# Router logits of two expert stages computed inside the preceding attention; flag rows written from two queues

## The reference, cut to what matters

```python
x = x + L0_xattn(layernorm(x), ctx, ctx)          # stage l0a: 16 heads of 16
x = x + L0_ffn(layernorm(x))                      # stage l0f: 8 experts, best one
x = x + L1_xattn(ctx, layernorm(x))               # alignment by dynamic programming
x = x + L1_ffn(layernorm(x))                      # stage l1f
x = x + L2_xattn(layernorm(x), ctx)               # stage l2a: rotary, 16 heads
x = x + L2_ffn(layernorm(x))                      # stage l2f: 8 experts, best two
x = x + L3_xattn(layernorm(x), ctx, ctx, topk=32) # stage l3a
x = x + L3_ffn(layernorm(x))                      # stage l3f: attention over flagged tokens

def expert_ffn(x, Wr, br, W1, b1, W2, b2):        # x: 2048 tokens, already normalised
    logits = x @ Wr + br                          # 2048 x 8: the router
    gates, idx = ...                              # softmax at the best one (l0f) or over the best two (l2f)
    for e in range(8):
        y_e = gelu(x @ W1[e] + b1[e]) @ W2[e] + b2[e]
    return sum of gate * y_e over the chosen experts
```

## Time and profile before

| what | value |
|---|---|
| time, median of 3 runs | 2520.89 us (2513.68 to 2522.03) |
| the profiled execution's own time | 2515.29 us |
| its span | 2513.5 us |
| mean granted TensorE clock | 0.819 of full |
| PE busy | 2020.0 us (80%) |
| PEld busy | 1639.0 us (65%) |
| DVE busy | 1603.9 us (64%) |
| ACT busy | 1173.2 us (47%) |
| POOL busy | 948.7 us (38%) |

### The profile page before, as it was taken

One profiled execution on the slowest core, in us unless ns is written; L12 is line 12 of the kernel. 1 busy time (PEld: TensorE's weight loads), 2 busy tenths in 40 slices (PEclk: granted clock), 3 DMA queues, 4 the chain that ended last, 5 costly groups with the idle time before them and its releaser, 6 DMA issues. The chain is left out here.

```text
span 2513.5 us, 40472 instructions
## 1 busy us (share of the span) xinstructions
PE 2020.0 (80%) x13332; PEld 1639.0 (65%) x13332; DVE 1603.9 (64%) x5245; ACT 1173.2 (47%) x3284; POOL 948.7 (38%) x906
## 2 busy tenths in 40 slices
PE   8995899599948967776999946777777877774887
PEld 5664798599837855555999935566666666662564
DVE  6765111588974246753111169999999999992784
ACT  3552232455321114432333326677787777771443
POOL 3310454300006023302555435666666666651110
PEclk9996899755879988987999966676777777777899
DMA  3111575520305012323454330010010000002342
GB/s 94 64 56 59 205 246 178 150 33 1 134 17 176 0 63 75 102 70 126 149 197 162 103 120 24 1 38 9 30 38 10 30 30 1 30 30 105 127 152 68
DMA packets 104533, 207.81 MB, mean 83 GB/s; under 512 B 20334, under 2 KB 72455, under 8 KB 96391
## 3 DMA queue, kind: packets, MB, share of 16 engines
q1 hardware_dynamic: 80520, 119.75, 14.5%
q0 software_dynamic: 23808, 85.50, 9.9%
HBM read 217.99 MB, written 56.92 MB: 109 GB/s over the span
## 5 line engine op out<-in xcount | busy, mean ns | idle before, releaser
L802 DVE MATCH_REPLACE8 l3a_left<-l3a_top,l3a_left 128x256 f32<-128x256 f32 x768 | 312.4, 420 | 0.0
L795 DVE MAX8 l3a_top<-l3a_left 128x8 f32<-128x256 f32 x768 | 289.5, 424 | 0.0
L507 POOL TENSOR_TENSOR l3a_prob<-l3a_expd,l3a_rest 128x512 f32<-128x512 f32 x128 | 162.5, 1270 | 208.3 <-ACT l3a_rest L589 207.4
L362 PEld LDWEIGHTS l3a_psO<-l3a_probT,l3a_vp 128*128 128x128 f32 x1024 | 177.6, 258 | 71.0 <-ACT l3a_probT L605 41.4
L362 PE MATMUL l3a_psO<-l3a_probT,l3a_vp 128*128 128x128 f32 x1024 | 201.3, 358 | 27.0 <-ACT l3a_probT L605 27.0
L344 PE MATMUL l3a_psT<-all_ident,l3a_prob 128*128 128x128 f32 x512 | 110.0, 354 | 109.6 <-POOL l3a_prob L507 109.0
L494 POOL TENSOR_TENSOR l3a_kept<-l3a_raw_sc,l3a_mone 128x512 f32<-128x512 f32 x128 | 163.2, 1275 | 70.6 <-ACT l3a_raw_sc L573 63.6
L1821 ACT ACTIVATE l2f_hT<-l2f_psH,l2f_wt 128x128 f32<-128x128 f32 x312 | 89.2, 368 | 213.3 <-PE l2f_psH L1752 213.3
L500 POOL TENSOR_TENSOR l3a_sc_sb<-l3a_kept,l3a_mlow 128x512 f32<-128x512 f32 x128 | 164.6, 1286 | 10.0
L2183 PE MATMUL dtw_psS<-dtw_r,all_shift 128*128 128x1 f32 x596 | 152.9, 357 | 10.1 <-DVE dtw_r L2363 9.7
L344 PEld LDWEIGHTS l3a_psT<-all_ident,l3a_prob 128*128 128x128 f32 x512 | 78.3, 182 | 126.5 <-POOL l3a_prob L507 126.3
(11 more groups left out here) (545 smaller groups left out, 4815.6 us busy)
## 6 DMA issues: line engine op xcount, KB each, us to landing
key_at<-l3a_a_k SPq DMA_DIRECT2D x8, 768.0 KB, 3.3
o_at<-l0a_oraw SPq DMA_DIRECT2D x16, 256.0 KB, 2.0
l0a_osum<-o_at SPq DMA_DIRECT2D x32, 128.0 KB
kv_at<-dtw_vd SPq DMA_DIRECT2D x8, 512.0 KB, 2.8
k_at<-dtw_kx SPq DMA_DIRECT2D x8, 512.0 KB, 4.0
l1f_kx<-k_at SPq DMA_DIRECT2D x8, 512.0 KB, 4.6
kv_at<-l1f_k SPq DMA_DIRECT2D x8, 512.0 KB, 3.2
l2a_k<-kv_at SPq DMA_DIRECT2D x8, 512.0 KB, 5.8
```

The lines of the kernel that those rows point to most:

```text
L362: mm = nc.tensor.matmul(psO[y % 2][:, c, 0:P], vp[:, p, kc, c, g * P:g * P + P], probT[:, u % 2, kc, e, :], start=(j == 0 and e == 0 and k ...
L507: nc.gpsimd.tensor_tensor(prob[:, u % 4, :, :], expd[:, u % 2, :, :], rest[:, u % 2, :, :], ALU.subtract).then_inc(picked, 1)
L795: ins = nc.vector.max(top[:, e, eight], rows[:, e, :] if r else scores[:, e, :])
L802: ins = nc.vector.match_replace(out=rows[:, e, :], in_to_replace=top[:, e, eight], in_values=rows[:, e, :] if r else scores[:, e, :], imm_ ...
```

## The change

Both `paired_attention` calls in front of an expert stage get `route`: shared tiles for mean and variance (`mv`) and raw logits (`lg_raw`), and the router's weights. Right behind `add_out` of batch g (slot 4g + 14) DVE makes the statistics of its two tiles and subtracts the mean (`row_moments`); in slot 4g + 15 PE turns the rows (`rows_turned`) and ACT copies them (`read_rows`); in slot 4g + 17 PE multiplies by the router's weights (`routed`) and DVE copies the 16 columns (`read_routes`). The loop becomes three slots longer, and the ring of banks gets the uses "fx" and "fl". The expert stage takes the root and reciprocal of all deviations at once, multiplies the raw logits by it and adds the bias; ACT makes the normalised rows from `x`, `rstd` and an offset; the gates are formed later. In l3f, `n_w` no longer counts the four small constants: they are issued ahead of batch 1's loads and waited for as `m_in`; `w_in` (with `wo`) is waited for by PE only in slot 14. In l3a the 16 flag DMAs are split between SP and ACT.

```diff
@@ picked_attention, sync / scalar
+        def flag_rows(queue, what, first, done):
+            parts = ahead[what].rearrange("b p (e c n) -> b p e c n", c=DC, n=S)
+            for f in range(2):
+                row = ahead["flags"][first + f:first + f + 1, :]....to_broadcast([B, P // 32, S])
+                for e in range(2):
+                    for c in range(DC):
+                        queue.dma_start(parts[:, DK * (1 - e) + 1 + f:P:32, e, c, :], row).then_inc(done, 16)
...
-            for what, f in (("q", 0), ("q", 1), ("k", 2), ("k", 3)):
-                for e in range(2):
...
-            sp.wait_ge(flagged, 16 * 17)
+            flag_rows(sp, "q", 0, q_flagged)
+            sp.wait_ge(q_flagged, 16 * 8)
...
+            act.wait_ge(flagged, 16)
+            act.wait_ge(a_out[(B - 1) % 2], 48 * (B // 2))
+            act.wait_ge(a_out[B % 2], 48 * (B // 2))
+            flag_rows(act, "k", 2, k_flagged)
+            act.wait_ge(k_flagged, 16 * 8)
@@ paired_attention
-    LAST = NQ + 11
+    LAST = NQ + (11 if route is None else 14)
...
-        n_w = 1 + len(Br) + (4 if groups is not None else 0)
+        n_w = 1 + len(Br)
...
+            if route is not None:
+                turns += [[], [("fl", (n - 17) // 4)], [], [("fx", (n - 15) // 4)]][t]
...
                 sp.dma_start(mk[:], groups[2:4, :]).then_inc(m_in, 16)
+                for n, t in (("sel", rg_sel), ("own", rg_own), ("fold", rg_fold), ("one", rg_one)):
+                    sp.dma_start(t[:], w[n]).then_inc(m_in, 16)
...
+            def rows_turned(g):
+                out = take("fx", g)
+                pe.wait_ge(xc_set, g + 1)
+                for c in range(DC):
+                    for t in range(QT):
+                        mm = nc.tensor.transpose(out[:, c, t * P:t * P + P], xc[:, t, c * P:c * P + P], ident[:])
+                mm.then_inc(fx_ps, 1)
+
+            def routed(g):
+                out = take("fl", g)
+                pe.wait_ge(fx_ev, g + 1)
+                if g == 0:
+                    pe.wait_ge(r_in, 16)
+                for t in range(QT):
+                    mm = product(out[:, 0, t * E:t * E + E], [xcT[:, c, t * P:t * P + P] for c in range(DC)], [wr_sb[:, c, :] for c in range(DC)])
+                mm.then_inc(fl_ps, 1)
...
-            pe.wait_ge(w_in, 16 * n_w)
-            if groups is not None:
-                pe.wait_ge(m_in, 16)
+            if groups is None:
+                pe.wait_ge(w_in, 16 * n_w)
             for n in range(LAST):
                 b, t = divmod(n, 4)
+                if groups is not None and n == 1:
+                    pe.wait_ge(m_in, 16 * 5)
+                if groups is not None and n == 14:
+                    pe.wait_ge(w_in, 16 * n_w)
...
+                if route is not None and t == 3 and 0 <= (n - 15) // 4 < B:
+                    rows_turned((n - 15) // 4)
+                if route is not None and t == 1 and 0 <= (n - 17) // 4 < B:
+                    routed((n - 17) // 4)
...
+            if made_at is not None:
+                pool.wait_ge(m_in, 16 * 5)
+                register_queries(0)
             pool.wait_ge(w_in, 16 * n_w)
-            if made_at is not None:
-                register_queries(0)
...
+            def read_rows(g):
+                act.wait_ge(fx_ps, g + 1)
+                if g:
+                    act.wait_ge(fl_ps, g)
+                nc.scalar.activation(xcT[:], bank_of("fx", g)[:], ACT.Copy).then_inc(fx_ev, 1)
...
+            def row_moments(g):
+                dve.wait_ge(x_done, g + 1)
+                if g:
+                    dve.wait_ge(fx_ps, g)
+                for t in range(QT):
+                    nc.vector.bn_stats(r_st[:, t, :], x[:, QT * g + t, :]).then_inc(r_stats, 1)
+                for t in range(QT):
+                    dve.wait_ge(r_stats, QT * g + t + 1)
+                    nc.vector.bn_aggr(mv[:, QT * g + t, :], r_st[:, t, :]).then_inc(r_moments, 1)
+                for t in range(QT):
+                    n = QT * g + t
+                    dve.wait_ge(r_moments, n + 1)
+                    last = nc.vector.tensor_scalar(xc[:, t, :], x[:, n, :], mv[:, n, 0:1], None, ALU.subtract)
+                last.then_inc(xc_set, 1)
+
+            def read_routes(g):
+                dve.wait_ge(fl_ps, g + 1)
+                nc.vector.tensor_copy(lg_raw[:, QT * g:QT * g + QT, :]..., bank_of("fl", g)[:, 0, 0:QT * E]).then_inc(lg_ev, 1)
...
-            dve.wait_ge(w_in, 16 * n_w)
+            if groups is None:
+                dve.wait_ge(w_in, 16 * n_w)
+            else:
+                dve.wait_ge(m_in, 16 * 5)
@@ moe
-            sp.dma_start(wr_sb[:], wr.rearrange("(c p) e -> p c e", p=P)).then_inc(w_in, 16)
...
-            pe.wait_ge(w_in, 32)
-            for t in range(NT + 1):
...
-            stats.root(act, 0)
-            for t in range(4):
-                read_t(t)
...
+            act.wait_ge(eps_set, 1)
+            nc.scalar.activation(std[:], mv[:, :, 1], ACT.Sqrt, bias=epst[:, 0:1]).then_inc(rooted, 1)
+            nc.scalar.activation(warm[:], epst[:], ACT.Exp)
+            act.wait_ge(off_set, 1)
+            for t in range(NT):
+                nc.scalar.activation(xn[:, t, :], x[:, t, :], ACT.Identity, bias=offset[:, t:t + 1], scale=rstd[:, t:t + 1]).then_inc(x_norm, 1)
...
-            for g in range(2):
-                stats.moments(dve, g)
-                dve.wait_ge(stats.done, g + 1)
...
+            dve.wait_ge(rooted, 1)
+            then(nc.vector.reciprocal(rstd[:], std[:]))
+            nc.vector.scalar_tensor_tensor(out=offset[:], in0=mv[:, :, 0], scalar=-1.0, in1=rstd[:], op0=ALU.mult, op1=ALU.mult).then_inc(off_set, 1)
+            then(nc.vector.tensor_tensor(lg[:], lg_raw[:], rstd[:].unsqueeze(2).to_broadcast([P, NT, E]), ALU.mult))
+            dve.wait_ge(w_in, 16)
+            then(nc.vector.tensor_tensor(lg[:], lg[:], br_sb[:].unsqueeze(1).to_broadcast([P, NT, E]), ALU.add))
```

More of the change, by code:

```diff
@@ L207, in picked_attention @@
                                "flagged", "step"))
+        q_flagged, k_flagged = s.sem("q_flagged"), s.sem("k_flagged")
         EARLY = NT - QT
+        def flag_rows(queue, what, first, done):
+            parts = ahead[what].rearrange("b p (e c n) -> b p e c n", c=DC, n=S)
+            for f in range(2):
+                row = ahead["flags"][first + f:first + f + 1, :].rearrange("o (b n) -> b o n", b=B).to_broadcast([B, P // 32, S])
+                for e in range(2):
+                    for c in range(DC):
+                        queue.dma_start(parts[:, DK * (1 - e) + 1 + f:P:32, e, c, :], row).then_inc(done, 16)
         block = s.block()
@@ L1077, in _ @@
                 load_made(2)
+            if route is not None:
+                sp.dma_start(wr_sb[:], route["wr"].rearrange("(c p) e -> p c e", p=P)).then_inc(r_in, 16)
             if given:
@@ L1492, in _ @@
                     read_values(y)
+                if route is not None and t == 3 and 0 <= (n - 15) // 4 < B:
+                    read_rows((n - 15) // 4)
                 if groups is not None and t == 1 and 0 <= b - 1 < B:
@@ L1634, in _ @@
                     register_mix((n - 13) // 4)
+                if route is not None and t == 1 and 0 <= (n - 17) // 4 < B:
+                    read_routes((n - 17) // 4)
                 if t == 2 and 0 <= (n - 14) // 4 < B:
                     add_out((n - 14) // 4)
+                if route is not None and t == 2 and 0 <= (n - 14) // 4 < B:
+                    row_moments((n - 14) // 4)
 F = 1024
 FC = F // P
-E = 8
 ROW_B1 = DC * F
@@ L1658, in __init__, with moe @@
         self.sem, self.base = sem, 0
-def moe(nc, dma, name, k_top, x, ident, rstd, mean, c, wr, br, table, rows_x, rows_y):
+def moe(nc, dma, name, k_top, x, ident, rstd, c, route, br, table, rows_x, rows_y):
     NB, KT = moe_blocks(k_top), k_top * NT
@@ L1909, in add_b2 @@
                 nc.vector.tensor_tensor(y[:, p, :], psY[p][:, 0:D], wt2[:, p, ROW_B2:ROW_B2 + D], ALU.add).then_inc(y_done, 1)
-            for g in range(2):
-                stats.moments(dve, g)
-                dve.wait_ge(stats.done, g + 1)
-                for t in range(*stats.tiles(g)):
-                    nc.vector.tensor_scalar(xn[:, t, :], x[:, t, :], mean[:, t:t + 1], rstd[:, t:t + 1],
-                                            ALU.subtract, ALU.mult).then_inc(x_norm, 1)
+            nc.vector.memset(epst[:], EPS).then_inc(eps_set, 1)
             nc.vector.memset(ones[:], 1.0)
@@ L1942, in _ @@
             ins.then_inc(hot_done, 1)
-            dve.wait_ge(exp_out, 1)
-            if k_top == 1:
-                then(nc.vector.tensor_reduce(gsum[:], ex[:], AX.X, ALU.add))
-                then(nc.vector.reciprocal(gate[:, 0, :], gsum[:]))
-            else:
-                then(nc.vector.tensor_scalar(gsum[:], ex[:, :, 0], 1.0, None, ALU.add))
-                then(nc.vector.reciprocal(gate[:, 0, :], gsum[:]))
```

(13 more changed lines are left out.)

65 lines of the change are left out of this document (21 added, 44 removed).

## The result

The changed kernel took 2493.01 us (median of 7 runs, 2486.31 to 2504.81), the kernel before beside it 2518.74 (7 runs, 2513.68 to 2522.03): ratio 0.9898, 95% interval 0.9875 to 0.9921, that is 20 to 31 us less. Run again with other kernels it gave 0.991 (0.9886 to 0.9934), 22.6 less.

What follows compares the result with a forecast made beforehand. Bounds: PE in lockstep with DVE in l0a, PE's load waits in l2a, the logits path before the experts, DMA issue ending l3a. Terms: l0 +4.0, l2 -3.7, l3 -13.6, total -13.3; predicted 2507.6 us, range 2494 to 2520.

Steps and rivals of the forecast that it cites:

- term 6: Start of l3f: DVE starts earlier, no longer waiting for `wo` and batch 1's loads: -8.4 us, bounds 0 and 9.
- term 3: Last batches: routing of batch 6 ahead of the dummy matmuls, plus 1.0 late routing: l0a +7.3, l2a +8.4 us.
- 4, router of the last batch: After the last addition in l0a and l2a, the last batch's moments, turning and routing: +4.6 us each.
- term 2: Router pieces in loaded slots: 2.1 plus 1.0 us a batch, l0a +14.5; l2a +5.7 after its waits.
- The wait absorbs them: In l2a, PE's load waits take added pieces: four waits of 8.8 us against 11.4 of work, 2.6 left.
- rival D: PE's clock falls in every batch from added waits: 15 to 22 us more, 2523 to 2530; chance 0.09.
- My own sign of being wrong: In the attention loops, the forecast is wrong if added pieces disappear or batches grow by more than 4 us.
- A: Moments cost only what PE itself does, in l0a and l2a: about -10 us, 2497.5; chance 0.13.
- B: At l3a's end and l3f's start, queues don't split or first loads interleave: 2513 to 2516; chance 0.15.
- C: Dummy matmuls in l0a and l2a run at low clock after batch 6's addition: +9.8 us, 2517.4; chance 0.11.
- Term 1: Front of the two expert stages: logits at 2.9 us instead of 25.3 after the start, -22.4 us each.
- Term 5: End of l3a: eight flag DMAs issued beside the other eight, -5.2 us; bound 0 if engines share one resource.

Runs made afterwards that it cites:

- e1: The kernel before with the l3 edits alone (flag DMAs from two queues, early start of l3f): ratio 0.9957 against the kernel before.
- e9: The kernel before with four buffers instead of three for l2a's keys and values, loads a batch earlier: ratio 0.9941 against the kernel before.
- e2: The changed kernel with both l3 edits undone, leaving the router inside the two attentions: ratio 0.9952 against the kernel before.
- e3: The changed kernel unaltered, run once more beside others: ratio 0.991 against the kernel before.
- e10: The changed kernel with four buffers instead of three for l2a's keys and values: ratio 0.9903 against the kernel before.
- e5: The kernel before with l2a's loads of keys and values issued one sum earlier, ahead of `realign`: ratio 1.0019 against the kernel before.
- e6: The changed kernel with l2a's loads issued one sum earlier, ahead of `realign`: ratio 0.9922 against the kernel before.
- e4: The changed kernel with turning and routing of batch 6 behind the output projection of batch 7: 2474.97 us, ratio 0.9840 against the kernel before.
- e7: e4 with moments, turning and routing of batches 0 to 4 in slots 4g+17, 4g+18 and 4g+19: ratio 0.9847 against the kernel before.

## Why the prediction was wrong

The sum by its own steps. Measured values are means over the profiles with the same code in that place: for the code before, before, e1 and, in l0 and l3, e9; for the router inside, the changed kernel, e2, e3 and, in l0 and l3, e10; for term 6, all kernels.

| term | forecast | measured |
|---|---|---|
| 1, front of the expert stages | -22.4 each | -24.1; -22.1 (whole stages l0f and l2f) |
| 2, router pieces in l0a, with the 1.0 of term 3 | +15.5 | +9.8 |
| 2, the same in l2a | +6.7 | +0.4 |
| 3, last two additions, l0a; l2a | +6.3; +7.4 | +6.7 (16.3 to 17.8 against 10.0); +7.6 |
| 4, router of the last batch | +4.6 each | +5.0; +5.1 |
| 5, flags | -5.2 | -4.2 |
| 6, start of l3f | -8.4 | -8.4 |

The measured terms add up to -24.2, the timed differences were -25.7 and -22.6. In l0 the code of e5 is that of the kernel before and the code of e6 that of the changed one; with them, term 2 in l0a is +10.7 instead of +9.8. From slot 12 on the terms were read off these stretches: 12 to 28, 28 to the addition of batch 6, from there to that of batch 7, and to the next stage; up to slot 12 nothing changed (l2a: 72.2 and 72.1 us).

**Term 2 failed, twice.** With the 1.0 of late routing that term 3 adds in each stage it was +22.2, and measured +10.2. These 12.0 us are more than the whole miss of the sum (-24.2 against -13.3); the other terms together came out 1.1 us the other way.

In l0a the sum was "5 x 2.1 + 4 x 1.0". The 1.0 was right (0.98). The 2.1 is 1.54: PE's wait is 0.88 instead of 1.45. The moments take 1.44 us, not 1.8, so the maxima come 1.07 us later (1.44 less the 0.37 of the earlier trace rows), and 0.19 of that PE had to spare. Slots 12 to 28, four moments and turnings and three routings, thus grew by 9.3 us (93.8 against 84.5) and not 11.4. The rest of the pieces, 4.1 us from slot 28 to the addition of batch 6, gave only 0.5 (44.15 against 43.6). I put that down to the sums' way through DRAM, which the addition waits for, as I had written under term 3, while still adding the PE work in front of it in full. The clock is at least as large a part. The windows view of this stretch in e5 and the kernel before (old code), then in e4 and the changed kernel (with the pieces):
```profile
158.50:198.02 39.52, 33.72 (x399) 21.23 (x396) 23.18 (x29) 21.14 (x41) 4.11 (x6) 1.00 0.22 75
...
158.91:201.84 42.93, 36.01 (x401) 22.06 (x398) 23.33 (x29) 21.25 (x41) 4.10 (x6) 0.96 0.21 69
...
166.40:209.07 42.67, 36.21 (x428) 24.08 (x425) 26.28 (x43) 22.30 (x43) 4.18 (x6) 1.00 0.20 69
...
167.23:211.40 44.17, 35.67 (x422) 24.05 (x418) 26.42 (x43) 22.29 (x43) 4.17 (x6) 0.96 0.19 67
```
At a clock of 1.00 on both sides the pieces cost 3.2 us (42.7 less 39.5), at 0.96 on both sides 1.2, from one pair of profiles each. The 0.5 comes from old-code profiles at 0.96, 0.92 and 0.88 set against new ones at 0.96. So this part of the small cost in l0a is in part luck of the clock; how much of the 4.1 was hidden by the DMAs stays open.

In l2a the step was "The wait absorbs them", four waits of 8.8 us against 11.4 of work, "What sticks out is 2.6". The mechanism is right and e9 shows it. The size missed two things: the work is 9.1 (e10 less e9), not 11.4, and the four waits were worth 11.8 us when e9 took them away, not 8.8. The earlier trace rows had it in front of me, a start in 2.09 us where 1.15 is normal after 4.76 of waiting, and I used it only against the change, as rival D. From slot 12 to 28 the stage became 2.2 us shorter with 9 us more work in it (82.3 against 84.5), where +2.6 was forecast. My own sign of being wrong, added pieces that disappear, came true here. From slot 28 to the addition of batch 6 it was +2.7 instead of +4.1; there, too, the clock differed (0.90 before, 0.92 to 1.00 after, in slots 28 to 32).

**The rivals.** D is refuted: l2a's clock is higher with the change, not lower, and l0a's batches grew by 2.52 us and no more. Its mechanism worked in the change's favour. The Trainium skill, TensorE: Matmul & The Clock Gate, section "HAM oscillation — how this bites in real kernels", says that waits in a loop cost TensorE its clock; the trace agrees, in the kernel before: 0.95 with the waits, 1.00 in e9 without. I had asked it of the waits that the change adds (0.88 us) and not of those that it removes (2 to 4.8 us). A comes closest in time, 2497.5, but not in cause: PE does wait for the moments. B is refuted, both queues issue at once and the constants land ahead of batch 1's loads. C too: the dummies took 8.6 and 9.1 us (8.5 to 10.2 in the other profiles with this order), neither 7.03 nor 13.1. Its ground was misread: of the eight records in l0f most took 1.06 us, but the last 0.59, as at full clock.

**Term 1** was right: from l0f's first instruction to its first fetch of weights it took 35.5 us before and 12.8 after, 22.7 less, and logits after 2.7 us, 2.9 forecast.

**Term 5** was 1.0 short. The eight issues into `q_at` in the kernel before:
```profile
2288.78 5.34 SPq L274 DMA_DIRECT2D q_at<-flags  x8
```
One after the other on SP they take 0.67 us each (5.34 / 8), and those into `key_at` 0.65; side by side it is 0.71 on SP (5.69 / 8) and 0.77 on ACT (6.12 / 8). ACT alone was not tried. From l3a's last work to l3f's first instruction it was 17.16 before and 12.95 after (e1: 12.83, e2: 17.12). The page that the prediction weighed (the Trainium skill, DMA: Bandwidth & Descriptors, section "Issuing engines are not separate DMA queues") grants a second issuer only the sequencers' time to issue, and calls it usually small beside the DMA. For DMAs this small the trace shows that time as the larger part of the stretch (10.6 of 17.16 us), and the second issuer gave 4.2 us, not the 0 of the warning.

**Term 6**: from its first instruction l3f took 205.0 to 208.7 us with the old start and in eight of nine kernels 197.0 to 203.2 with the new one (193.6 in e7). DVE starts 8.5 us after the first load of keys instead of 15.5. PE's own start at 2300.39 gave nothing for itself: at 2304.53 it had waited again, for the same constant as DVE.

**Left open.** Kernels with the same code differ by up to 9 us in l3a and by 4 in the last batches of l0a. The traces show slots at either clock there (1.00 over the last batches of l0a in e5, 0.88 in e1, the same code); what sets it in one execution and not in another was not tried. Each run has one profile, so a term that is smaller than this scatter is only as good as the two to four profiles behind each of its sides. Nor was the dummies' place tried with the router of batch 6 behind them but ahead of the projection.

## What to carry over

Before pricing work that is added to a pipelined loop, list the loop's waits and take them away in a kernel of their own (a deeper buffer): it shows what the loop is worth without them, and whether a gain that comes later is new or these same microseconds. Don't price a wait at its length alone: here four of 8.8 us were worth 11.8, with a clock of 0.95 beside them. And compare stretches of two kernels at the same clock: 39.5 and 44.0 us of the same code (e5, e1) differ by more than the pieces that were to be priced there. Work of the next-to-last batch belongs behind anything that fills the last wait: here that order alone cost 15 us, more than half of what the change gained.

## What was not expected of the hardware

Two loads of 512 KB (one batch's keys and values), issued just ahead of a 256 KB store, made it 5.4 to 6.5 us instead of 2.0 to 2.8 until the store was done and the loads back could go (e5 and the kernel before, slots 12 to 28 of l2a). Two engines can issue small DMAs side by side at little loss: on SP an issue took 0.71 us instead of 0.67, while ACT took 0.77.
